# Query and key parts by feature in DRAM: three transfers for a group of four heads in place of six

## Time and profile before

| | |
|---|---|
| median of 3 runs | 578.76 us (577.4 to 581.91) |
| profiled execution, its own time | 579.01 us |
| its span | 576.6 us, mean granted clock of TensorE 0.914 |
| PE busy | 474.7 us, 82% |
| DVE busy | 398.2 us, 69% |
| ACT busy | 291.6 us, 51% |
| POOL busy | 219.4 us, 38% |
| DMA | 35295 packets, 45.48 MB, 79 GB/s over the span |

### The profile page before, as it was taken

One profiled execution on the slowest core, in us unless ns is written; L12 is line 12 of the kernel. 1 busy time (PEld: TensorE's weight loads), 2 busy tenths in 40 slices (PEclk: granted clock), 3 DMA queues, 4 the chain that ended last, 5 costly groups with the idle time before them and its releaser, 6 DMA issues. The chain is left out here.

```text
span 576.6 us, 6249 instructions
## 1 busy us (share of the span) xinstructions
PE 474.7 (82%) x1925; PEld 200.1 (35%) x1925; DVE 398.2 (69%) x641; ACT 291.6 (51%) x509; POOL 219.4 (38%) x210
## 2 busy tenths in 40 slices
PE   8999356697987768989889869797988878798885
PEld 3433221142431213354333314453422333243454
DVE  5899968835678597537797896569647757732285
ACT  2146320145476383724758755436776523677434
POOL 6566666533067586231558783223000001000000
PEclk9999875588997899989989999989989978898898
DMA  7476324111278511111765203120311110000011
GB/s 228 159 191 178 106 86 136 36 36 37 83 194 200 110 55 57 56 37 64 184 155 128 57 3 90 55 66 1 106 46 42 57 36 3 1 1 1 1 36 36
DMA packets 35295, 45.48 MB, mean 79 GB/s; under 512 B 5920, under 2 KB 29120, under 8 KB 35264
## 3 DMA queue, kind: packets, MB, share of 16 engines
q1 hardware_dynamic: 32144, 38.02, 23.0%
q10 hardware_dynamic: 3120, 7.08, 4.9%
HBM read 34.93 MB, written 9.96 MB: 78 GB/s over the span
## 5 line engine op out<-in xcount | busy, mean ns | idle before, releaser
L1396 DVE TENSOR_REDUCE MX<-bank 128x1 f32<-128x512 f32 x256 | 166.8, 681 | 123.4 <-PE bank L574 120.8
L1046 ACT ACTIVATE PT<-bank 128x512 f32<-128x512 f32 x256 | 146.7, 598 | 138.8 <-PE bank L583 131.3
L574 PE MATMUL bank<-KS,QS 96*128 96x512 bf16 x232 | 91.5, 399 | 37.4 <-DVE MX L1396 27.3
L583 PE MATMUL bank<-QS,KS 99*128 99x512 bf16 x256 | 100.8, 405 | 14.8 <-ACT PT L1046 14.3
L1712 POOL TENSOR_TENSOR W<-qT,W 128x512 f32<-128x512 f32 x48 | 61.8, 1289 | 40.6 <-DVE W L1315 26.6
L597 PE MATMUL bank<-PT,Vs 128*32 128x512 f32 x512 | 74.4, 655 | 1.8 <-ACT PT L1046 0.8
L583 PEld LDWEIGHTS bank<-QS,KS 99*128 99x128 bf16 x256 | 24.4, 99 | 102.8 <-issue 52.4
L574 PEld LDWEIGHTS bank<-KS,QS 96*128 96x128 bf16 x232 | 22.9, 99 | 94.3 <-DVE MX L1396 59.7
L1698 POOL TENSOR_TENSOR W<-kT,W 128x512 f32<-128x512 f32 x32 | 46.3, 1450 | 6.6 <-ACT kT L904 6.6
L1743 POOL TENSOR_TENSOR MP<-MX,zero 128x16 bf16<-128x16 f32 x15 | 4.9, 324 | 101.9 <-issue 52.7
L1536 DVE TENSOR_TENSOR_SCAN W<-bank,W 128x512 f32<-128x512 f32 x32 | 38.8, 1218 | 2.5 <-DVE W L1521 0.2
(11 more groups left out here) (213 smaller groups left out, 729.6 us busy)
## 6 DMA issues: line engine op xcount, KB each, us to landing
W<-v_rows SPq DMA_DIRECT2D x12, 512.0 KB, 6.4
W<-v_rows ACTq DMA_DIRECT2D x12, 512.0 KB, 6.3
KS<-k_parts SPq DMA_DIRECT2D x96, 64.0 KB, 2.3
QS<-q_parts SPq DMA_DIRECT2D x96, 64.0 KB, 2.4
k_parts<-parts SPq DMA_DIRECT2D x9, 256.0 KB, 2.1
q_parts<-parts SPq DMA_DIRECT2D x9, 256.0 KB, 2.8
cT<-in_cT SPq DMA_DIRECT2D x4, 512.0 KB, 3.5
xtok<-in_x SPq DMA_DIRECT2D x4, 512.0 KB, 7.7
```

The lines of the kernel that those rows point to most:

```text
L574: pe.matmul(bank(n)[:, :], QS[0:NS, h, i * P:(i + 1) * P], KS[0:NS, h, :], start=True, stop=True).then_inc(filled(n), 1)
L583: pe.matmul(bank(name)[:, :], KS[0:NR, h, kt * P:(kt + 1) * P], QS[0:NR, h, :], start=True, stop=True).then_inc(filled(name), 1)
L1046: act.activation(PT[:, n % 2, j, :], bank(name)[:, :], ACT.Exp).then_inc(emptied(name), 1)
L1396: dve.tensor_reduce(MX[:, NT * h + i:NT * h + i + 1], bank(n)[:, :], AX.X, ALU.max).then_inc(emptied(n), 1)
```

## The change

`k_parts` and `q_parts` change from (sequence, part, half, 128, 512) to (sequence, part, feature, head, 512), so that four heads of one feature are 4 KB in one piece. The slots are reordered so that equal query parts and rising key parts are neighbours: the keys' slots hold parts 0, 1, 2, 0, 1, 0 and the queries' 0, 0, 0, 1, 1, 2, which gives the same six pairs. A group of keys comes with three transfers, of parts 0 to 2, 0 to 1 and 0, to 48, 32 and 16 partitions. A group of queries comes with three as well, in which one part is read three times, twice and once, by a broadcast in front. The stores in the steps are made half by half: two of 128 KB for a part in place of one of 256 KB; in the prologue they were by halves already. The counts of the semaphores follow.

```diff
-SLOTS_K = [0, 0, 1, 1, 0, 2]
-SLOTS_Q = [0, 1, 0, 1, 2, 0]
+SLOTS_K = [(0, 3), (3, 2), (5, 1)]
+SLOTS_Q = [(0, 0, 3), (3, 1, 2), (5, 2, 1)]
...
+            def keys_of(b, g, at, parts_in):
+                src = t["k_parts"][b, 0:parts_in, :, 4 * g:4 * g + 4, :].rearrange("p d h n -> p d (h n)")
+                sp.dma_start(KS[HD * at:HD * (at + parts_in), 4 * g:4 * g + 4, :], src).then_inc(K_in[g], 16)
+
+            def queries_of(b, g, at, part, times):
+                src = t["q_parts"][b, part, :, 4 * g:4 * g + 4, :].rearrange("d h n -> d (h n)")
+                sp.dma_start(QS[HD * at:HD * (at + times), 4 * g:4 * g + 4, :],
+                             src.unsqueeze(0).broadcast_to([times, HD, 4 * S])).then_inc(Q_in[g], 16)
+
+            def part_out(dram, b, p, m, done):
+                dst = t[dram][b, p].rearrange("d (m h) n -> m h d n", m=ND)[m]
+                sp.dma_start(dst, parts[:, p, m, :]).then_inc(done, 16)
...
             def queries_in(b, g):
-                sp.wait_ge(Q_out, count(48, b, 48))
+                sp.wait_ge(Q_out, count(96, b, 96))
...
-                for s, part in enumerate(SLOTS_Q):
-                    heads = t["q_parts"][b, part, g // 2].rearrange("(h d) n -> d h n", d=HD)
-                    sp.dma_start(QS[HD * s:HD * s + HD, 4 * g:4 * g + 4, :],
-                                 heads[:, 4 * (g % 2):4 * (g % 2) + 4, :]).then_inc(Q_in[g], 16)
+                for query_slots in SLOTS_Q:
+                    queries_of(b, g, *query_slots)
...
                     for p, part in enumerate((Q_hi, Q_mid, Q_lo)):
                         sp.wait_ge(part, count(1, o, 1))
-                        sp.dma_start(t["q_parts"][o, p].rearrange("t p n -> p t n"), parts[:, p, :, :]).then_inc(Q_out, 16)
+                        for m in range(ND):
+                            part_out("q_parts", o, p, m, Q_out)
...
-                    pe.wait_ge(Q_in[h // 4], count(96, b, 96))
+                    pe.wait_ge(Q_in[h // 4], count(48, b, 48))
...
-        t[name] = nc.dram_tensor(name, (B, 3, ND, P, S), BF16, kind="Internal").ap()
+        t[name] = nc.dram_tensor(name, (B, 3, HD, H, S), BF16, kind="Internal").ap()
```

More of the change, by code:

```diff
@@ L26 @@
 RQ = DV // 4
-NS = 16 * len(SLOTS_K)
+NS = 16 * 6
 NR = NS + 3
@@ L281, in build @@
         x1_done = sem("x1_done"); x1b_done = sem("x1b_done")
-        K_hi = sem("K_hi", 1); K_r1 = sem("K_r1", 1); K_mid = sem("K_mid", 1); K_lo = sem("K_lo", 1); K_out = sem("K_out")
-        Q_hi = sem("Q_hi", 1); Q_r1 = sem("Q_r1", 1); Q_mid = sem("Q_mid", 1); Q_lo = sem("Q_lo", 1); Q_out = sem("Q_out")
+        K_hi = sem("K_hi", 1); K_r1 = sem("K_r1", 1); K_mid = sem("K_mid", 1); K_lo = sem("K_lo", 1); K_out = sem("K_out", 48)
+        Q_hi = sem("Q_hi", 1); Q_r1 = sem("Q_r1", 1); Q_mid = sem("Q_mid", 1); Q_lo = sem("Q_lo", 1); Q_out = sem("Q_out", 48)
         K_in = [sem(f"K_in{g}") for g in range(NG)]
@@ L389, in keys_in @@
+            def part_out(dram, b, p, m, done):
+                dst = t[dram][b, p].rearrange("d (m h) n -> m h d n", m=ND)[m]
+                sp.dma_start(dst, parts[:, p, m, :]).then_inc(done, 16)
             def keys_in(b, g):
                 sp.wait_ge(ks_set, 3)
-                sp.wait_ge(K_out, count(48, b, 48))
+                sp.wait_ge(K_out, count(96, b, 96))
                 sp.wait_ge(*full_of(f"s{4 * g + 3}.2", b - 1))
                 sp.wait_ge(*full_of(f"s{4 * g + 3}.3", b - 1))
[L395 to L398, removed]
+                for key_slots in SLOTS_K:
+                    keys_of(b, g, *key_slots)
@@ L429, in prologue @@
                 sp.wait_ge(K_hi0, 1)
-                first_parts("k_parts", 0, 0, parts[:, 0, 0, :], K_out0)
+                part_out("k_parts", 0, 0, 0, K_out0)
                 sp.wait_ge(K_hi0, 2)
-                first_parts("k_parts", 0, 1, parts[:, 0, 1, :], K_out)
+                part_out("k_parts", 0, 0, 1, K_out)
                 sp.wait_ge(K_mid0, 1)
-                first_parts("k_parts", 1, 0, parts[:, 1, 0, :], K_out0)
+                part_out("k_parts", 0, 1, 0, K_out0)
                 sp.wait_ge(K_mid0, 2)
-                first_parts("k_parts", 1, 1, parts[:, 1, 1, :], K_out)
+                part_out("k_parts", 0, 1, 1, K_out)
                 sp.wait_ge(K_lo0, 1)
-                first_parts("k_parts", 2, 0, parts[:, 2, 0, :], K_out0)
+                part_out("k_parts", 0, 2, 0, K_out0)
                 sp.wait_ge(K_lo0, 2)
-                first_parts("k_parts", 2, 1, parts[:, 2, 1, :], K_out)
+                part_out("k_parts", 0, 2, 1, K_out)
                 sp.wait_ge(K_out0, 48)
-                first_in(KS, "k_parts", SLOTS_K, 0, K_in)
-                first_in(KS, "k_parts", SLOTS_K, 1, K_in)
+                for key_slots in SLOTS_K:
+                    keys_of(0, 0, *key_slots)
+                for key_slots in SLOTS_K:
+                    keys_of(0, 1, *key_slots)
                 sp.wait_ge(x1_done, count(NT, 0, NT))
@@ L446, in prologue @@
                 sp.wait_ge(Q_hi0, 1)
-                first_parts("q_parts", 0, 0, parts[:, 0, 0, :], Q_out0)
+                part_out("q_parts", 0, 0, 0, Q_out0)
                 sp.wait_ge(Q_mid0, 1)
-                first_parts("q_parts", 1, 0, parts[:, 1, 0, :], Q_out0)
+                part_out("q_parts", 0, 1, 0, Q_out0)
                 sp.wait_ge(Q_lo0, 1)
-                first_parts("q_parts", 2, 0, parts[:, 2, 0, :], Q_out0)
+                part_out("q_parts", 0, 2, 0, Q_out0)
                 sp.wait_ge(Q_out0, 48)
-                first_in(QS, "q_parts", SLOTS_Q, 0, Q_in)
-                first_in(QS, "q_parts", SLOTS_Q, 1, Q_in)
+                for query_slots in SLOTS_Q:
+                    queries_of(0, 0, *query_slots)
+                for query_slots in SLOTS_Q:
+                    queries_of(0, 1, *query_slots)
                 sp.wait_ge(Q_hi0, 2)
-                first_parts("q_parts", 0, 1, parts[:, 0, 1, :], Q_out)
+                part_out("q_parts", 0, 0, 1, Q_out)
                 sp.wait_ge(Q_mid0, 2)
-                first_parts("q_parts", 1, 1, parts[:, 1, 1, :], Q_out)
+                part_out("q_parts", 0, 1, 1, Q_out)
                 sp.wait_ge(Q_lo0, 2)
-                first_parts("q_parts", 2, 1, parts[:, 2, 1, :], Q_out)
-                sp.wait_ge(K_out, 48 + FIRST)
-                sp.wait_ge(Q_out, 48 + FIRST)
+                part_out("q_parts", 0, 2, 1, Q_out)
+                sp.wait_ge(K_out, 96 + FIRST)
+                sp.wait_ge(Q_out, 96 + FIRST)
                 for g in (2, 3):
-                    first_in(KS, "k_parts", SLOTS_K, g, K_in)
-                    first_in(QS, "q_parts", SLOTS_Q, g, Q_in)
+                    for key_slots in SLOTS_K:
+                        keys_of(0, g, *key_slots)
+                    for query_slots in SLOTS_Q:
+                        queries_of(0, g, *query_slots)
             prologue()
@@ L481, in _ @@
                         sp.wait_ge(part, count(1, o, 1))
-                        sp.dma_start(t["k_parts"][o, p].rearrange("t p n -> p t n"), parts[:, p, :, :]).then_inc(K_out, 16)
+                        for m in range(ND):
+                            part_out("k_parts", o, p, m, K_out)
                     keys_in(o, 0)
@@ L512, in _ @@
             sp.wait_ge(v_out, 16 * B + FIRST)
-            sp.wait_ge(K_out, 48 * B + FIRST)
-            sp.wait_ge(Q_out, 48 * B + FIRST)
+            sp.wait_ge(K_out, 96 * B + FIRST)
+            sp.wait_ge(Q_out, 96 * B + FIRST)
         @block.tensor
@@ L569, in max_tile @@
                 if h % 4 == 0 and i == 0:
-                    pe.wait_ge(K_in[h // 4], count(96, b, 96))
-                    pe.wait_ge(Q_in[h // 4], count(96, b, 96))
+                    pe.wait_ge(K_in[h // 4], count(48, b, 48))
+                    pe.wait_ge(Q_in[h // 4], count(48, b, 48))
                 n = f"m{h}.{i}"
@@ L700, in first_max @@
                 if i == 0 and h % 4 == 0:
-                    pe.wait_ge(K_in[h // 4], count(96, 0, 96))
-                    pe.wait_ge(Q_in[h // 4], count(96, 0, 96))
+                    pe.wait_ge(K_in[h // 4], count(48, 0, 48))
+                    pe.wait_ge(Q_in[h // 4], count(48, 0, 48))
                 n = f"m{h}.{i}"
@@ L975, in gated_end @@
                     act.wait_ge(*read("K1", o))
-                    act.wait_ge(Q_out, count(48, o, 0))
+                    act.wait_ge(Q_out, count(96, o, 0))
                     act.activation(parts[:, 0, :, :], full32[:, :, :], ACT.Copy).then_inc(K_hi, 1)
@@ L995, in gated_end @@
                     act.wait_ge(*read("Q1", o))
-                    act.wait_ge(K_out, count(48, o, 48))
+                    act.wait_ge(K_out, count(96, o, 96))
                     act.activation(parts[:, 0, :, :], full32[:, :, :], ACT.Copy).then_inc(Q_hi, 1)
@@ L1218, in prologue @@
                 second_part("Q", 0, Q_mid0)
-                act.wait_ge(K_out, 48 + FIRST)
+                act.wait_ge(K_out, 96 + FIRST)
```

## The result

The changed kernel takes 593.32 us (median of 4 runs, 589.25 to 598.24) against 580.34 us (median of 4, 577.4 to 583.86): ratio 1.025, 95% interval 1.0189 to 1.0312. It is slower by some 2.5%. The interval lies clear of 1. Forecast were 587.4 us and a range of 577 to 599. The profiled execution took 593.02 us with a span of 591.2 us, 14.6 more than before.

What follows compares the result with a forecast made beforehand. No single engine bounds the kernel; what delays PE's list in order delays all. Terms 3.3 + 1.4 + 2.5 + 1.4 = 8.6 us on the profiled 579.0 gave 587.6, by the median 587.4; range 577 to 599.

Steps and rivals of the forecast that it cites:

- the four places named: First use of query group 0 in prologue and steps 0 to 2: later by 3.3, 1.4, 2.5, 1.4 us.
- over 9.5 had been named as a sign: Prologue: PE idle by over 9.5 us before the first maxima tile would show the forecast.
- Two and three engines, the same ones each time: Query loads by broadcast use three, then two engines, the first shared: 33 rows on it for a group.
- The first rival: Query loads use sixteen engines after all and step 0's 2.75 us stall goes: 575.0 us, chance 0.15.
- the second: Rival: keys also cut by two or three parts, delaying query stores and context in the steps: 598.0 us, chance 0.15.
- the price of a group on the first engine: Query group load: 33 rows of 4 KB at 0.165 us plus fixed 2.1 us, 7.5 us; upper end 9.9.
- The fixed part of 2.1 us: Share of a load's time apart from its rows, from the context's load: 3.4 - 8 x 0.165 us.
- Stores: Stores by halves over eight engines: last lands 0.8 us later (0 to 1.2), in the prologue 0.4.
- The clock: PE's clock falling in a stall: nothing put on for it.
- third rival: Three engines, but stalls of steps 0 to 2 made up again: prologue's 3.3 us alone, 582.1 us, chance 0.08.

Runs made afterwards that it cites:

- the feature turned outermost: Changed kernel, with feature outermost and slot inside in the partitions of key and query loads, same three transfers; 575.6 us, ratio 0.9989 to the kernel before.
- the pair made single: Changed kernel, with only the second query transfer (one part read twice) made as two of 16 partitions; 583.5 us, ratio 1.0103 to the kernel before.
- keys by broadcast: Changed kernel, with queries in three transfers joined over parts and keys in three by broadcast; 584.1 us, ratio 1.0168 to the kernel before.
- changed, feature outermost in the stores: Changed kernel, with query and key weight columns permuted so stores have 16 features outermost, not 8 heads; 590.9 us, ratio 1.0227 to the kernel before.

## Why the prediction was right, and where its sizes were off

**What bounds.** Right: the four places named are those where most of the time went. The first tile of group 0 came later by 5.8 us in the prologue (93.6 against 87.8), 8.9 in step 0 (201.5, 192.6), 11.4 in step 1 (324.5, 313.1) and 16.7 in step 2 (438.5, 421.75). PE was idle for 12.2 us before the first of them; over 9.5 had been named as a sign.

**Two and three engines, the same ones each time.** Right, and shown: 42 completions for two groups, the feature turned outermost (all of the loss gone), the pair made single (2.0 us for 14 rows). The second window of step 2 bears it out as well: two engines are still busy at 440 us, 8.3 us after the first packet. Were the pair or the second group on other engines, none would have had more than 34 rows, which is 5.4 us. The Trainium skill's rule on a broadcast in front (DMA: Bandwidth & Descriptors, Rules for kernel authors) is what these runs show, with 3 and 2 completions for three and two copies; which engines they are by number no run here shows. The first rival, sixteen engines, is out. So is the second for this kernel: the keys' transfers came over 16 engines, with 48 completions for a group; its mechanism, keys on few engines ahead of the query stores and of the context, is what the run with keys by broadcast shows, at most of its price (9 us by the ratios of 1.0168 and 1.001, 7.3 by the spans of the two profiles; the rival had 10.6).

**The term that was mis-sized** is the first one, the price of a group on the first engine: 7.5 us forecast, 9.1 measured. About as much was missing at all four places: step 2 took 9.1 too, and in steps 0 and 1 the forecast had 10.5 and 11.8 us from first issue to tile, measured were 12.2 and 13.7. The row was right (0.165 forecast; 0.16 from the windows of step 2, 0.14 from the pair). The fixed part of 2.1 us, taken from the context's load, was not: 9.1 less 33 rows of 0.16 leaves 3.8. Part of that lies before the first packet. The DMA view's strip of busy tenths over the 3 us from just before the first issue (40 slices of 0.075 us), changed kernel in step 2 from 429.4, and in the prologue from 84.4:

```profile
DMA  0000000000000000000000000000000403079111
```

```profile
DMA  0000000000000000000009000000003021211206
```

Feature outermost, from 416.5:

```profile
DMA  0000000000000000000965345995999799019962
```

Before, from 414.7:

```profile
DMA  0000000000002263363259531269830024673334
```

The first packet comes 2.3 us after the issue in step 2 where the broadcast is in front, 1.4 where 16 features are outermost, 0.9 before. But the 2.3 is not fixed: in the prologue it is 1.6, as it is with the pair made single, and the prologue's group took 9.1 us all the same. The context's load had its first packet after some 1.0. So 0.6 to 1.3 of the missing 1.7 us lie there, and where the rest goes no run shows. It is paid once for each group that is waited for.

**Stores.** The prologue's loads began 1.3 us later (84.46 against 83.19) where 0.4 was forecast. Of this, 0.4 is that the stores themselves began later and took longer to issue; from the last issue to the first load it is 2.2 us against 1.4. With 16 features outermost in the stores it is 1.8, so eight engines cost the 0.4 forecast, and the rest has another cause that stays open. By this and the term above the prologue cost 5.8 in place of 3.3, step 0 cost 3.1 more in place of 1.4, step 1 2.5 as forecast. That last agreement is luck: PE stood still there for 4.92 us, and before not at all, but the 329 matmuls between the start of step 1 and that tile took 2.8 us less than before (75.77 against 78.60), at a granted clock of 1.00 against 0.96.

**The clock.** I put nothing on for a clock that falls in a stall. Windows from the first tile in step 1 to the start of step 2, changed kernel and, below, before (length, busy us of PE, PEld, DVE, ACT, POOL, granted clock, DMA share, GB/s):

```profile
324.53:359.31 34.78, 29.01 (x133) 9.25 (x133) 28.82 (x39) 19.99 (x34) 24.30 (x21) 0.90 0.10 30
```

```profile
313.10:345.57 32.47, 25.92 (x133) 8.84 (x132) 28.72 (x39) 21.61 (x36) 25.98 (x23) 1.00 0.10 26
```

The same 133 matmuls take 3.1 us longer at 0.90 of the full clock (2.4 GHz, with stretches at 1.2), and the stretch 2.3. With the 3.0 us by which the next stretch, with step 2's own stall of 3.23, is longer, that is the 5.3 by which its first tile moved, where 1.4 was forecast. Cut finer, the changed kernel's trace shows when the clock fell:

```profile
320.00:324.53 4.53, 0.00 (x0) 0.03 (x1) 0.00 (x0) 1.37 (x2) 1.21 (x1) 1.00 0.23 80
324.53:328.00 3.47, 3.47 (x12) 1.01 (x13) 2.87 (x3) 0.46 (x1) 0.97 (x1) 0.51 0.13 51
328.00:345.00 17.00, 15.16 (x77) 6.16 (x76) 12.65 (x18) 11.67 (x21) 12.09 (x10) 1.00 0.18 51
345.00:359.31 14.31, 10.39 (x47) 2.08 (x45) 13.31 (x20) 7.86 (x14) 11.24 (x12) 0.88 0.00 1
```

Right behind the stall of 4.92 us PE works at 1.2 GHz for some 3.5 us, with 12 matmuls where the kernel with a stall of 2.79 us at this place (changed, feature outermost in the stores) gets 16 done in the same time at 1.00:

```profile
325.79:329.30 3.51, 3.51 (x16) 1.24 (x17) 2.94 (x3) 1.08 (x2) 1.20 (x1) 1.00 0.14 56
```

That is the term the prediction put at nothing. The second slow stretch, after 345, comes 20 us later, and kernels with no stall in step 1 have one too (feature outermost: 0.95 over the 33 us from this tile), so about half of the 3.1 us goes with the stall. In step 3 it is the other way round:

```profile
467.14:561.60 94.46, 77.18 (x364) 34.46 (x362) 48.88 (x98) 51.40 (x93) 7.03 (x18) 0.95 0.05 15
```

```profile
449.62:547.00 97.38, 81.50 (x364) 35.91 (x362) 49.06 (x98) 51.40 (x93) 7.03 (x18) 0.89 0.05 15
```

2.9 us less with a higher clock, in a step with no group 0 to wait for. So the clock moves the parts of one execution by 2 to 3 us either way, and beyond the stretch behind the stall no cause is shown for it.

**Stalls that are made up again** (third rival): out. What each place lost was still missing at the next, but for the 2.8 us of clock in step 1.

**Sum.** 5.8 + 3.1 + 2.5 + 5.3 - 2.1 (from step 2's first tile to the end) = 14.6 us on the profiled executions; by the medians 13.0, by the ratio 14.5. Forecast 8.6. The misses are 2.5, 1.7, 0 and 3.9 at the four places and -2.1 at the end: the mechanism was right, its price was put too low, and that the end and step 1 gave time back is luck.

**A version that beats both?** With the feature outermost the three transfers cost no more than the six: ratio 0.9989 (0.995 to 1.003). That undoes the loss and gains nothing that can be measured; the only stall in the steps that it shortens is step 0's, from 2.75 to 2.06 us.

## What to carry to other kernels

Count the completions of a transfer in the trace before trusting its size: fewer and bigger rows help nothing when the outermost count of one side leaves two or three engines to move them, and a broadcast in front does just that. Where the partition order is free, put the dimension of 16 outermost and the repetition inside; it costs one rearrangement. And a transfer confined to few engines is not hidden because its own data are early: what stands behind it on the first engine's queue may be what is waited for.

## What the runs showed of the hardware that was not expected

A transfer by a broadcast of three in front put its first packet on the way 1.6 us after its issue in the prologue and 2.3 us in step 2, against 0.9 for a plain one of 16 partitions, so it is late before it is slow. Keys on three engines delayed stores that use eight by some 3 us, with 4.6 us of issue in between. PE's granted clock fell to 1.2 GHz right behind a stall of 4.92 us and stayed at 2.4 behind one of 2.79 at the same place of another run. The length alone does not decide it: in step 2 of that run, behind 2.82 us, the first tile's matmul took 0.55 us and not 0.38.
